# Last stage of a language-model tower: rows transposed by DMA, two rows each for VectorE and ScalarE, four buffers, no loop

## What is computed

```python
xn = layernorm(h)                                     # per token
x_scale = max(abs(xn).max() / 127, 1e-5)              # one number over all tokens
x_int8 = clip(round(xn / x_scale), -128, 127)
out = h + (x_int8 @ weight_int8.T) * x_scale * weight_scale.T + bias
```

## Time and profile before

| | |
|---|---|
| three runs | 1285.45, 1287.5, 1288.92 us; median 1287.5 |
| the profiled execution | 1287.84 us; its span 1286.0 us |
| last stage, from the first rounding (1234.17 us) to the end of the span | 51.8 us |
| busy over the whole span | PE 89%, DVE 87%, ACT 61%, POOL 56% |
| busy in 1245 to 1275 us | DVE 100%, ACT 100%, PE 85%, DMA engines 53% |

### The profile page before, as it was taken

The page is one execution under the profiler, slowest core; times in us unless marked ns, Lnnn a source line. Parts: engine busy times, 40 slices in busy tenths (PEclk is TensorE's granted clock), DMA queues, the critical chain, the costliest instruction groups (busy, mean ns, idle before and its releaser), DMA issues. The chain is left out here.

```text
span 1286.0 us, 25011 instructions
## 1 busy us (share of the span) xinstructions
PE 1149.3 (89%) x7285; PEld 761.0 (59%) x7292; DVE 1112.5 (87%) x1994; ACT 789.0 (61%) x1275; POOL 715.1 (56%) x2062
## 2 busy tenths in 40 slices
PE   2991075999999999999999999999999999999987
PEld 1550032567676757676666667675767676667554
DVE  5998989979898989898989899998989897887188
ACT  4666747384848484748484757666575747452358
POOL 8882010747585858585858585858575766650000
PEclk9999997899999999999999999999999999999999
DMA  9999901010101010101010100000000101000015
GB/s 354 408 407 418 417 21 36 1 36 1 36 1 36 2 35 0 35 2 34 3 32 8 27 13 22 18 17 18 17 19 16 28 7 34 3 19 1 1 66 196
DMA packets 37169, 91.60 MB, mean 71 GB/s; under 512 B 10173, under 2 KB 21778, under 8 KB 32770
## 3 DMA queue, kind: packets, MB, share of 16 engines
q1 hardware_dynamic: 33474, 81.32, 17.9%
q0 software_dynamic: 3072, 8.39, 1.7%
q10 hardware_dynamic: 576, 1.31, 0.3%
HBM read 81.29 MB, written 9.70 MB: 71 GB/s over the span
## 5 line engine op out<-in xcount | busy, mean ns | idle before, releaser
L804 POOL TENSOR_TENSOR stp<-Gs,X 128x32 f32<-128x32 f32 x900 | 262.7, 292 | 263.1 <-ACT X L777 196.2
L806 POOL TENSOR_TENSOR Gs<-Gs,stp 128x32 f32<-128x32 f32 x900 | 274.4, 305 | 70.4
L1215 PE MATMUL bank<-w_fc,gl 128*128 128x256 f32 x1024 | 242.6, 383 | 0.1
L1196 PE MATMUL bank<-mT,w_fc 128*128 128x512 f32 x512 | 236.7, 595 | 1.8 <-ACT mT L1176 1.7
L1215 PEld LDWEIGHTS bank<-w_fc,gl 128*128 128x128 f32 x1024 | 191.6, 191 | 54.5 <-issue 27.0
L654 PE MATMUL bank<-xT,w_in 128*128 128x512 f32 x448 | 207.3, 603 | 9.0 <-DVE uT L1104 8.9
L966 ACT ACTIVATE uT<-bank,cols 128x512 f32<-128x512 f32 x64 | 47.9, 775 | 224.6 <-DVE sz L1111 134.8
L1196 PEld LDWEIGHTS bank<-mT,w_fc 128*128 128x128 f32 x512 | 94.9, 190 | 85.9 <-issue 79.9
L654 PEld LDWEIGHTS bank<-xT,w_in 128*128 128x128 f32 x448 | 81.8, 191 | 93.1 <-issue 77.8
L980 DVE SCALAR_TENSOR_TENSOR uT<-bank,cols,uT 128x500 f32<-128x500 f32 (+1 forms) x192 | 133.4, 733 | 2.3
L359 DVE TENSOR_TENSOR peak<-ring,peak 128x1536 f32<-128x1536 f32 (+2 forms) x67 | 115.3, 1721 | 9.0 <-ACT ring L258 6.8
(11 more groups left out here) (220 smaller groups left out, 1897.5 us busy)
## 6 DMA issues: line engine op xcount, KB each, us to landing
ring<-in_table SPq DMA_DIRECT2D x31, 1536.0 KB
d_rep<-d_rows SPq DMA_DIRECT2D x128, 64.0 KB, 2.0
out<-res SPq DMA_DIRECT2D x14, 512.0 KB, 2.9
b_rep<-bc_rows SPq DMA_DIRECT2D x128, 32.0 KB, 1.8
c_rep<-bc_rows SPq DMA_DIRECT2D x128, 32.0 KB, 1.8
w_fc<-in_w_fc SPq DMA_DIRECT2D x2, 1024.0 KB, 15.1
ring<-in_table SPq DMA_DIRECT2D x2, 768.0 KB
w_in<-in_w_in ACTq DMA_DIRECT2D x1, 1088.0 KB
```

The lines of the kernel that those rows point to most:

```text
L804: pool.tensor_tensor(stp[:], Gs[:, t, ::-1, :], X2[:, t, :, :], ALU.mult).then_inc(rec.sem, 1)
L806: pool.tensor_tensor(Gs[:, t + 1, :, :], Gs[:, t, :, :], stp[:], ALU.add).then_inc(rec.sem, 1)
L1196: last = pe.matmul(pj[n % 4][:, :], w_fc1[:, k, n * P:(n + 1) * P], mT[:, k, :], start=(k == 0), stop=(k == KD - 1))
L1215: last = pe.matmul(sbk[j // 2][:, (j % 2) * D:(j % 2 + 1) * D], gl[n % LEAD][:, j * LEN:(j + 1) * LEN], w_fc2[:, n, :], start=False, stop= ...
```

## The change

Transposing `whole` no longer uses PE and ACT. SP issues a DMA transpose per group, from `whole` to `wholeT`, both in SBUF; `turned` (one semaphore for each of four buffers) tells when it has landed. `whole`, `wholeT` and `res` have four buffers, `back` is doubled by taking the two banks that held the transposed rows. DVE centres two sequences of a group and ACT two. DVE rounds four groups ahead of its adding. All loops are written out. PE gets matmuls with unused results (`spare`): twelve at the start, three in each group from the third on.

```diff
+            BUF = 4
+            DROWS = 2
+            AHEAD = 4
-            whole = [tmp(f"whole{i}", [P, G, D], BF16) for i in range(2)]
-            wholeT = [tmp(f"wholeT{i}", [P, KD, TOK], BF16) for i in range(2)]
+            whole = [tmp(f"whole{i}", [P, G, D], BF16) for i in range(BUF)]
+            wholeT = [tmp(f"wholeT{i}", [P, G, KD, LEN], BF16) for i in range(BUF)]
-            res = [tmp(f"res{i}", [P, G, D]) for i in range(4)]
+            res = [tmp(f"res{i}", [P, G, D]) for i in range(BUF)]
-            DROWS = G - 1
+            acc = [bank[2:4], bank[4:6]]
+            back = [bank[6:8], bank[0:2]]
...
             def _(sp):
+                def turn_in(g):
+                    if g >= BUF:
+                        sp.wait_ge(acc_mm.sem, acc_mm.at(g - BUF))
+                    sp.wait_ge(rounded.sem, rounded.at(g))
+                    sp.dma_start(wholeT[g % BUF][:].rearrange("p j k t -> p (j k) t"),
+                                 whole[g % BUF][:].rearrange("p j c -> p (j c)"),
+                                 transpose=True).then_inc(turned[g % BUF], 16)
+                for g in range(GROUPS):
+                    turn_in(g)
+                    if g >= AHEAD:
+                        store(g - AHEAD)
...
             def _(pe):
+                def spare(g, n):
+                    for _ in range(n):
+                        pe.matmul(acc[g % 2][0][:, :], ident_b[:], w_q[:].rearrange("p k c -> p (k c)"),
+                                  start=True, stop=True, skip_group_check=True)
+                def multiply(g):
+                    pe.wait_ge(turned[g % BUF], nth(g))
+                    if g >= 2:
                         pe.wait_ge(accT_ready.sem, accT_ready.at(g - 2))
...
+                def turn_back(g):
                     pe.wait_ge(accT_ready.sem, accT_ready.at(g))
+                    if g >= 2:
+                        pe.wait_ge(res_ready.sem, res_ready.at(g - 2))
...
+                spare(0, 12)
+                multiply(0)
+                multiply(1)
+                for g in range(2, GROUPS):
+                    turn_back(g - 2)
+                    spare(g, 3)
+                    multiply(g)
+                turn_back(GROUPS - 2)
+                turn_back(GROUPS - 1)
...
             def _(act):
+                for g in range(AHEAD):
+                    centre(g)
+                for g in range(GROUPS):
+                    scale(g)
+                    if g + AHEAD < GROUPS:
+                        centre(g + AHEAD)
...
             def _(dve):
+                def round_rows(g):
                     for j in range(DROWS):
...
+                    if g >= BUF:
+                        dve.wait_ge(turned[g % BUF], nth(g - BUF))
+                    dve.wait_ge(rq.sem, rq.at(g))
                     for n in range(2):
-                        dve.wait_ge(rq.sem, rq.at(g, min(DROWS, 2 * n + 2)))
                         if n:
                             dve.wait_ge(centred.sem, centred.at(g))
...
+                for g in range(GROUPS):
+                    round_rows(g)
+                    if g >= AHEAD:
+                        add_rows(g - AHEAD)
+                for g in range(GROUPS - AHEAD, GROUPS):
+                    add_rows(g)
```

More of the change, by code:

```diff
@@ L1622, in build @@
             rounded = signal("rounded", 2)
-            whole_T = signal("whole_T", 1)
-            wT_ready = signal("wT_ready", 1)
+            turned = [sem(f"turned{i}") for i in range(BUF)]
             acc_mm = signal("acc_mm", KD)
@@ L1734, in _, with centre @@
+                turn_back(GROUPS - 2)
+                turn_back(GROUPS - 1)
             @block.scalar
             def _(act):
-                def centre(g, b, i):
-                    if later(i):
+                def centre(g):
+                    if g >= 2:
                         act.wait_ge(rounded.sem, rounded.at(g - 2))
-                    act.activation(f32q[b][:, G - 1, :], rows(g, G - 1), ACT.Identity,
-                                   bias=off_q[:, bass.ds(g * G + G - 1, 1)],
-                                   scale=rs_q[:, bass.ds(g * G + G - 1, 1)]).then_inc(centred.sem, 1)
@@ L1743, in take_T @@
-                def take_T(g, b, i):
-                    if later(i):
-                        act.wait_ge(acc_mm.sem, acc_mm.at(g - 2))
-                    act.wait_ge(whole_T.sem, whole_T.at(g))
-                    act.activation(wholeT[b][:].rearrange("p k t -> p (k t)"), bank[b][:, :].bitcast(BF16),
-                                   ACT.Copy).then_inc(wT_ready.sem, 1)
-                def scale(g, b, i):
-                    if later(i):
+                    for j in range(DROWS, G):
+                        s = g * G + j
+                        last = act.activation(f32q[g % 2][:, j, :], rows(g, j), ACT.Identity,
+                                              bias=off_q[:, s:s + 1], scale=rs_q[:, s:s + 1])
@@ L1753, in scale @@
+                    last.then_inc(centred.sem, 1)
+                def scale(g):
+                    if g >= 2:
                         act.wait_ge(out_T.sem, out_T.at(g - 2))
@@ L1810, in round_rows, with add_rows @@
                         s = slice(2 * n, 2 * n + 2)
[L1811 removed]
+                        dve.tensor_scalar(whole[g % BUF][:, s, :], f32q[g % 2][:, s, :], MAGIC, MAGIC,
                                           ALU.add, ALU.subtract).then_inc(rounded.sem, 1)
[L1814 to L1816 removed]
+                def add_rows(g):
+                    if g >= BUF:
+                        dve.wait_ge(stored[g % BUF], nth(g - BUF))
@@ L1817, in add_rows @@
                     for n in range(2):
                         dve.wait_ge(out_T.sem, out_T.at(g, n + 1))
-                        dve.tensor_tensor(res[b + 2 if fresh else b][:, 2 * n:2 * n + 2, :].rearrange("p j c -> p (j c)"),
-                                          bank[6 + n][:, :], rows(g, 2 * n, 2), ALU.add) \
+                        dve.tensor_tensor(res[g % BUF][:, 2 * n:2 * n + 2, :].rearrange("p j c -> p (j c)"),
+                                          back[g % 2][n][:, :], rows(g, 2 * n, 2), ALU.add) \
```

128 lines of the change are left out of this document (18 added, 110 removed).

## The result

The changed kernel takes 1288.62 us in the median of 12 runs (1286.97 to 1292.76), the kernel before, in the same comparison, 1286.82 (12 runs). The ratio is 1.0018, with a 95% interval of 1.0010 to 1.0026: 1.3 to 3.3 us slower. That is less than the 0.3% named at the start as what two times need to be told apart; the interval comes from 12 runs on each side. The prediction was 1283.7 us, a gain of 3.85. The time lies in the range of 1281.5 to 1299, on the other side of no change.

The account below looks back on a forecast made before the run. DVE was taken to set the pace. Gains of 3.2 (roundings), 1.2 (add) and 0.2 (start), less 0.05 (tail) and 0.7 (clock), make 3.85 us: from 1287.5 to 1283.7, with 8 in 10 between 1281.5 and 1299.

Parts of the forecast that it names:

- I take 1.0, the row with the smaller pieces: DMA engines: a 256 KB transpose takes 1.0 us of all engines, with 0.77 and 2.6 kept as ends.
- landing of 2.45: DMA transpose: lands 2.45 us after its group's rounding ends, from 1.35 fixed, 1.0 data and 0.1 waits.
- R: End of the last rounding on DVE, 1275.65 in the kernel before; 10.35 us follow it to the end of the span.
- The DMA engines become the bound: Rival, loop: a transpose above 1.09 us slows 12 groups from the fifth on; 1292.2 to 1301.8 us; chance 0.28.
- X: Engine time of one DMA transpose in us; with a store of 1.55 a group costs 1.55 + X.
- about 6: Loop: a transpose's landing could grow to about 6 us before DVE waits, as DVE rounds four groups ahead.
- Tail: Behind R: DVE's adds end 6.0 later, the store queue is late next and ends at R + 10.4, against 10.35.
- DVE per group: Loop: one f32q goes but whole waits for the one ahead; gain 0.20 us, period 2.64, bounds 0 to 0.32.
- One more add behind R: DVE rounds four ahead, so 11 adds and not 12 lie before R: R comes 1.20 us earlier.
- clock case: Start: PE waits for the first landing, its clock may fall to 0.5, costing 1 to 2.4 us; half a chance, 0.7.
- SP's holding: Rival, SP's queue: a transpose's issue holds SP 1.83 us, not 0.37; 1285.2 us, pace set from 2.26; chance 0.20.
- Block after block: Rival, DMA: a group's eight 128x128 blocks follow each other, 10.8 us per transpose, about 1430 us; chance 0.06.

Follow-up runs that it names:

- stores_quarter: Changed kernel, but stores of groups 0 to 13 write one sequence of four (128 KB, not 512); ratio 0.9975 to the kernel before.
- turn_half: Changed kernel, but each DMA transpose turns only two of four sequences (128 KB, not 256), zeros in the rest; ratio 0.9984 to the kernel before.
- pe_all_3b: Changed kernel with all transposes on TensorE, one multiply earlier, copied by ACT; three rounding rows on DVE, one on ACT; ratio 1.0012 to the kernel before.
- spare_28: Changed kernel with 28 spare matmuls at the start in place of 12; ratio 0.9996 to the kernel before.
- after: The changed kernel itself, against the kernel before: 1288.62 us in the median, ratio 1.0018.
- pe_all: Changed kernel with all transposes on TensorE right ahead of their own multiply, copied by ACT, two rows each for DVE and ACT; ratio 1.0133 to the kernel before.
- pe_all_3: Changed kernel with all transposes on TensorE right ahead of their own multiply; three rows on DVE, one on ACT; ratio 1.0097 to the kernel before.
- stores_pool: Changed kernel with whole stores of groups 0 to 13 issued by GpSimd in place of SP; ratio 1.0050 to the kernel before.

## Why the prediction was wrong, point by point

**The step that failed: "I take 1.0, the row with the smaller pieces", and with it the landing of 2.45 and the tail of R + 10.4.** A transpose costs the engines 1.24 (by the rate) to 1.42 us (by the share), both over the 1.09 that the prediction had named as the limit (1.16 at the period of 2.71 that came) and well inside its bounds of 0.77 to 2.6. It lands after 3.1 to 3.3 us alone and after up to 5.8 beside the stores. Both halves of that are shown: take bytes from the stores (stores_quarter) or from the transposes (turn_half), and the tail falls by 2.8 or 2.0 us.

**The rival that came nearest had the wrong place.** "The DMA engines become the bound" expected every group from the fifth on to cost 1.55 + X, with DVE idle in the loop. DVE never waited there: four buffers took up the growing landing, as the sentence on "about 6" said they would. The delay came out once, behind R, when there is nothing left to round. At X of 1.24 to 1.42 the rival's own price, 12 x (X - 1.09), is 1.8 to 4.0 on top of 1283.7.

**Tail.** Predicted: DVE's adds end at R + 6.0 and the store queue is late next. Measured: the adds end at R + 10.6, and 3.3 us of stores follow. PE was late next, by the landing of 5.77 and then by its own 2.39 a group, with three multiplies still to come. The prediction counted data for the stores here and did not follow groups 13 to 15 through landing, multiply, scale and turn_back. Its 2.55 for PE's group had turn_back at its duration, 1.04; by starts it is 0.87 (1277.80 to 1278.67), so the group is 2.39. That error made the tail look longer and not shorter.

**DVE per group.** Direction and most of the size were right: -0.13 (2.84 to 2.71), where -0.20 was forecast. The 0.77 held for the first roundings; 0.06 to 0.07 more came where `whole` waits for two semaphores. Over 12 groups that is 0.8 us. pe_all_3b has the same step (1.08 in the first group, 1.15 from the fifth on) with `whole_T` in the place of `turned` as the added semaphore. No kernel tried this wait by itself, so the cause is not shown.

**One more add behind R, and ACT.** The add moved as predicted, and ACT's group is 2.31 against 2.30, by the starts here:

```profile
1246.38 1.09 ACT L1724 ACTIVATE f32q<-h,off_q,rs_q 128x256 f32<-128x256 f32 x2
1247.37 1.43 ACT L1733 ACTIVATE accT<-bank,q_cols 128x512 f32<-128x512 f32 x2
1248.69 1.09 ACT L1724 ACTIVATE f32q<-h,off_q,rs_q 128x256 f32<-128x256 f32 x2
```

**Start and clock.** The clock case was right in kind: it fell, and the first two multiplies took 3.38 us. Landing and clock together made a wait of 1.57, where 0.5 was taken and 0.7 set aside: 0.4 too little. spare_28, whose clock held there, waited 0.94, so 0.6 of it is the clock's.

**The sum.** The stage was to fall by 3.85 and rose by 1.0, a miss of 4.9: tail 3.5, two-semaphore waits 0.8, start 0.4, and 0.2 not assigned. By the ratio the loss is 1.3 to 3.3 us. About 0.4 of it lies outside the span from the first to the last instruction: time less span is 2.13 to 2.27 us in the 12 runs of after, and 1.75 to 1.85 in the runs of the kernel before that stand beside the experiments. It doesn't go with the DMA transposes, since pe_all, without any, has 2.24 in the median, while pe_all_3 and pe_all_3b, with three `f32q` on DVE, have 1.8; why is open, and so is what else the loss has above the stage's 1.0.

**Other rivals.** SP's holding was long, 1.23 to 2.20. The 2.26 at which it would set the pace counted a store's issue at 0.37; with the medians that came, 1.71 and 0.69, SP was used 2.40 of 2.71 us, close to the limit and below it. In stores_quarter the holding fell with the load of the engines, and taking the stores off its queue didn't help. "Block after block" fell: eight blocks land together in 3.1 us. So the 1309 ns for a 128x128 transpose by DMA of the Trainium skill, "VectorE: DVE Perf Modes", section "The three transpose paths", are not a price per block here.

## What to carry to other kernels

When work moves to the DMA engines, add up the engines' time of all transfers in a period, with the moved one at its worst bound; if the sum comes within a few per cent of the period, as 2.55 of 2.64 us did here, reckon with a backlog. Here the buffers hid it in the loop and handed it over at the end: follow the last groups step by step through every engine behind R, for there each latency counts. Before comparing two tails, look at the granted clock in each: in spare_28 it made up 1.5 us. A mixed plan can keep some of the gain: here, DMA for the middle groups, and TensorE for the first two and last three (pe_ends_b, 0.9982 of the time before, 0.9972 to 0.9992).

## What the runs showed of the hardware

A DMA transpose of 256 KB from SBUF to SBUF moved 212 GB/s, where stores reached 346. The Trainium skill, "DMA: Bandwidth & Descriptors", section "Latency and other measured facts", gives 261 GB/s for a non-contiguous middle dimension and 350 to 400 for contiguous data; at 261 this transpose would, as an estimate, take 1.0 us and fit. The measurement decides: it doesn't.

SP was held about 1.2 us by a transpose of 128 KB as by one of 256 KB (1.21 and 1.23), and up to 4.36 when the engines were full (stores_pool, share 1.16). A store's issue took 0.37 us on a queue without transposes (the kernel before and pe_all_3b), 0.58 between transposes where the engines had room (stores_quarter and turn_half), and 0.69 in after. Stores from GpSimd's software queue made transposes land later (up to 9.2 us) than stores from the same queue as theirs (5.8).

PE's granted clock was 0.50 soon after a wait of 2.15 us in spare_28, where PE had been busy before; after the wait of 1.80 us in the tail of after it stayed at 1.00.
